# One float32 attention and mixture-of-experts layer: the first routed tile moved between two shared downs, and high-part products merged to 512 columns

## The reference, cut to what matters

```
x = x + attention(layernorm(x))
xt = layernorm(x).reshape(2048, 256)
topk_w, topk_i = top_k(sigmoid(xt @ w_router.T), 2)       # weights divided by their sum
gate = silu(einsum('th,eih->tei', xt, wg))
up = einsum('th,eih->tei', xt, wu)
expert_out = einsum('tei,ehi->teh', gate * up, wd)
out = einsum('te,teh->th', comb, expert_out)              # comb holds the weights
sgate = silu(einsum('th,jih->tji', xt, sg))
out = out + einsum('tji,jhi->th', sgate * einsum('th,jih->tji', xt, su), sd)
x = x + out
```

## Time and profile before

| | us |
|---|---|
| time, median of 3 runs | 905.71 (905.21 to 905.88) |
| the profiled execution | 906.11 |
| its span, first to last instruction | 904.4 |
| PE busy in the span | 870.5 (96%) |
| ACT, DVE, POOL busy | 578.6, 450.7, 276.2 |

### The profile page before, as it was taken

How to read it: one execution, slowest core, us unless ns; L and a number is a source line. 1 busy time by engine, 2 the same in 40 slices (tenths; PEclk the granted TensorE clock), 3 DMA queues, 4 the chain that set the end, 5 groups by cost and what they waited for, 6 DMA issues and landing times.

```text
span 904.4 us, 22574 instructions
## 1 busy us (share of the span) xinstructions
PE 870.5 (96%) x8167; PEld 561.6 (62%) x8168; DVE 450.7 (50%) x776; ACT 578.6 (64%) x733; POOL 276.2 (31%) x423
## 2 busy tenths in 40 slices
PE   8989999999999999999999999999999999999994
PEld 5524444433434343343447888888888989999983
DVE  8644443344444334454548677667834343434332
ACT  4789999999999999999993433342222222222220
POOL 5043334333333433333340000000024454544442
PEclk9979999999999999999999999999999999999998
DMA  6345444665544466733102206100037875575421
GB/s 189 122 132 185 151 164 164 218 214 210 193 154 162 161 219 228 244 99 90 31 13 76 70 27 240 50 1 24 1 101 217 269 226 160 158 205 154 121 36 23
DMA packets 42062, 124.43 MB, mean 138 GB/s; under 512 B 7668, under 2 KB 23028, under 8 KB 35824
## 3 DMA queue, kind: packets, MB, share of 16 engines
q1 hardware_dynamic: 31152, 110.35, 35.9%
q0 software_dynamic: 7072, 9.72, 6.0%
q10 hardware_dynamic: 3744, 3.02, 1.0%
HBM read 74.03 MB, written 49.02 MB: 136 GB/s over the span
## 4 chain that ended last, share of the span: by engine, by line
PE 79%; ACT 13%; issue 4%; DVE 2%; DMA 1%; POOL 0%; ACTq 0%; POOLq 0%; DVEq 0%
PE ps L1737 18%; PE ps L1910 14%; PE ps L1690 13%; PE ps L1864 12%; ACT arena L958 12%; PE ps L1932 7%; PE ps L1877 6%; PE ps L1921 2%; PE ps L1631 2%; PE ps L1791 2%; PE ps L1891 1%; DMA out<-arena,now_to 0%; PE ps L1821 0%; DMA xres<-x 0%; PE ps L1851 0%
## 5 line engine op out<-in xcount | busy, mean ns | idle before, releaser
L958 ACT ACTIVATE arena<-ps 128x1024 f32<-128x1024 f32 x336 | 319.9, 1063 | 2.0 <-PE ps L1690 2.0
L1737 PE MATMUL ps<-arena 128*32 128x256 f32 x4096 | 265.6, 386 | 0.6 <-POOL arena L785 0.6
L785 POOL TENSOR_SCALAR_AFFINE_SELECT arena<-arena 128x512 f32<-128x512 f32 x240 | 150.1, 638 | 265.7 <-ACT arena L969 258.0
L1690 PE MATMUL ps<-arena 64*128 64x512 bf16 (+1 forms) x1280 | 176.9, 343 | 12.1 <-ACT arena L958 8.5
L1737 PEld LDWEIGHTS ps<-arena 128*32 128x32 f32 x4096 | 112.4, 110 | 99.1 <-issue 42.4
L1690 PEld LDWEIGHTS ps<-arena 64*128 64x128 bf16 x1280 | 57.7, 94 | 157.9 <-ACT arena L958 79.5
L1189 DVE COPY_PREDICATED ps<-keep,ps 128x512 f32<-128x512 int32 (+1 forms) x128 | 80.6, 629 | 143.8 <-PE ps L1690 143.8
L1910 PE MATMUL ps<-wr_all,x2T 128*128 x648 | 141.3, 362 | 2.0 <-issue 1.0
L1910 PEld LDWEIGHTS ps<-wr_all,x2T 128*128 128x128 f32 x648 | 106.7, 189 | 19.5 <-issue 4.1
L1864 PE MATMUL ps<-x2T,wr_all 128*128 128x512 f32 x480 | 116.8, 394 | 1.3 <-issue 1.2
L969 ACT ACTIVATE arena<-ps 128x1024 f32<-128x1024 f32 x112 | 112.4, 1062 | 0.5 <-PE ps L1690 0.4
(11 more groups left out here) (198 smaller groups left out, 706.1 us busy)
## 6 DMA issues: line engine op xcount, KB each, us to landing
w_scr<-wr_all SPq DMA_DIRECT2D x24, 1280.0 KB, 7.3
wr_all<-w_scr SPq DMA_DIRECT2D x24, 1280.0 KB, 6.1
raw<-w_experts SPq DMA_DIRECT2D x24, 640.0 KB, 7.8
arena<-q_scr SPq DMA_DIRECT2D x64, 64.0 KB
o_scr<-arena SPq DMA_DIRECT2D x128, 32.0 KB, 1.7
arena<-o_scr SPq DMA_DIRECT2D x16, 256.0 KB, 4.0
raw<-w_shared SPq DMA_DIRECT2D x6, 640.0 KB, 5.0
q_scr<-parts SPq DMA_DIRECT2D x8, 384.0 KB, 3.0
```

What stands on the lines that cost most here:

```text
L785: nc.gpsimd.affine_select(out=dst, in_=src, compare_op=ALU.is_ge if own else ALU.is_gt, fill=0.0, base=0, pattern=[[0, REP], [-1 if own el ...
L958: nc.scalar.activation(prob[:, SLOT[unit(a, kt)], :, :].rearrange("p h q -> p (h q)"), score.rearrange("p b x -> p (b x)"), ACT.Exp, scale ...
L1690: return nc.tensor.matmul(ps[:, bank, :].rearrange("p (h q) -> p h q", h=2)[:, :, place * P:(place + tiles) * P], kst[r0:r0 + HALF, s, kt ...
L1737: last = nc.tensor.matmul(ps[32 * h:32 * h + 32, 6 + qc, a % 2 * QW:(a % 2 + 1) * QW], vst[:, s, kt, :], prob[:, SLOT[k], h, :], start=(no ...
```

## The change

- **Merged products.** In piece 2 (`SUMMED` = 1024 is its first column) and in the downs, the high activation part is multiplied with both weight parts in one product of 512 columns, whose moving operand is two pieces of 256 columns; the results lie side by side in the bank. The low activation part is multiplied with the high weights first, into the left half. So of three products of 256 columns one of 256 and one of 512 are left. The two halves are added on DVE: `up_sum` copies the left half to SBUF and adds the right one, for which `up` is cut in two; `y_out` scales the left half and then adds the scaled right half. The last tile's piece 2 and the last two tiles' downs stay as they were.
- **The first tile.** Pieces 0 to 2 of tile 0 and xT(1) stand between shared down(8) and down(9). Its hidden rows are turned into banks 3 and 6, since 4 and 5 still hold the shared downs; PE waits for the shared adds (`s_out`) only before hT(1). ACT's and DVE's steps for it move ahead too: DVE does `up` of tile 0 before it adds the last shared downs. `gact` and `hid` of parity 0 lie in another place of SBUF.
- **Chunk 0.** DVE copies the second half of the turned rows' high part, ACT only the first.
- **The last tile.** Piece 1 signals by itself, so `gate` can start before piece 2; `up` is cut in two with a wait for piece 2 between; the transposes signal in two parts.
- **POOL's `add`** waits for the scaled rows after it has staged the row numbers, read its count and waited for earlier adds. The pairs of ACT, DVE and POOL are written out, as PE's are.

```diff
             def add(j, i, p, n):
-                pool.wait_ge(e_y, j + 1 + FIRST)
                 stage(now_to[:, p:p + 1], slot_to[:, ds(j, 1)], n)
                 after = pool.value_load(tile_after[0:1, ds(j, 1)], min_val=16, max_val=16 * (NTILE // 2 + 1))
                 wait_apart(pool, e_added[1 - p], after)
+                wait_apart(pool, e_y, j + 1 + FIRST)
...
-            pairs = for_pairs(pool, 2, pair_rows)
...
             def x2_out(c):
                 act.wait_ge(c_tp, c + 1)
-                for k in range(KD):
+                for k in range(KD if c else 1):
                     nc.scalar.copy(x2T[:, 0, k, ds(c * CT, CT)], ps[:, XT_BANK[c] + k, :]).then_inc(c_xT, 1)
...
                     nc.scalar.activation(gsh[:, q % 2, :], ps[:, 2 * (q % 2), :], ACT.Silu).then_inc(s_act, 1)
+                    if step == NC * STEPS - 1:
+                        xT_out(0, 0)
                     act.wait_ge(s_hid, step + 1 + FIRST)
...
@@ -993,26 +998,28 @@
...
+            def hT_out(j, p):
+                act.wait_ge(e_th, j + 1)
+                if isinstance(j, int) and j == 0:
+                    nc.scalar.copy(hidT[:, 0, 0, 0:4].rearrange("p k t -> p (k t)"), ps[:, 3, :])
+                    nc.scalar.copy(hidT[:, 0, 0, 4], ps[:, 6, 0:P]).then_inc(e_hThi, 1)
+                    return
...
-            j = for_pairs(act, 1, pair) * 2 + 2
+            j = for_pairs(act, 1, pair, True) * 2 + 2
...
             gate(j + 1, 1)
-            act.wait_ge(e_th, j + 2)
             for i, (k0, k1) in enumerate(LAST_PARTS):
+                act.wait_ge(e_th, j + (2 + i))
...
+                if c == 0:
+                    nc.vector.tensor_copy(x2T[:, 0, 1, 0:CT], ps[:, XT_BANK[c] + 1, :]).then_inc(c_xT, 1)
...
+                    if step == NC * STEPS - 1:
+                        xT_low(0, 0)
...
                 if c == NC - 1:
-                    xT_low(0, 0)
+                    xT_low(1, 1)
+                    up_sum(0, 0)
+                    up(0, 0)
...
             def up(j, p):
                 dve.wait_ge(e_act, j + 1)
-                nc.vector.tensor_tensor(hid[:, p, :], gact[:, p, :],
-                                        ps[:, 0:3, :].rearrange("p b n -> p (b n)")[:, I:2 * I], ALU.mult) \
-                    .then_inc(e_hid, 1)
+                n = SUMMED - I
+                nc.vector.tensor_tensor(hid[p][:, 0:n], gact[p][:, 0:n], ps[:, 1, I - 512:I - 512 + n], ALU.mult)
+                dve.wait_ge(e_sum, j + 1)
+                nc.vector.tensor_tensor(hid[p][:, n:I], gact[p][:, n:I], hid[p][:, n:I], ALU.mult).then_inc(e_hid, 1)
+            def up_sum(j, p):
+                dve.wait_ge(e_gu, j + 1)
+                nc.vector.tensor_copy(hid[p][:, SUMMED - I:I], ps[:, 2, 0:2 * I - SUMMED]).then_inc(e_half, 1)
+                dve.wait_ge(e_half, j + 1)
+                nc.vector.tensor_tensor(hid[p][:, SUMMED - I:I], hid[p][:, SUMMED - I:I],
+                                        ps[:, 2, 2 * I - SUMMED:2 * (2 * I - SUMMED)], ALU.add).then_inc(e_sum, 1)
...
+                if isinstance(j, int) and j == 0:
+                    nc.vector.tensor_tensor(hidT[:, 0, 1, 0:4].rearrange("p k t -> p (k t)"), ps[:, 3, :],
...
-            def y_out(j, p):
+            def y_out(j, p, halves=False):
                 dve.wait_ge(e_mm, j + 1 + FIRST)
                 wait_apart(dve, y_free, j + 1)
+                if halves:
+                    nc.vector.tensor_scalar(ysb[:, p, :], ps[:, 6, 0:D], slot_w[:, ds(j, 1)], None, ALU.mult).then_inc(e_main, 1)
+                    dve.wait_ge(e_main, j + 1)
+                    nc.vector.scalar_tensor_tensor(out=ysb[:, p, :], in0=ps[:, 6, D:2 * D], scalar=slot_w[:, ds(j, 1)],
+                                                   in1=ysb[:, p, :], op0=ALU.mult, op1=ALU.add).then_inc(e_y, 1)
+                    return
...
             def routed_pair(i):
                 for p in range(2):
                     j = i * 2 + p
                     hT_low(j, p)
+                    up_sum(j + 1, 1 - p)
                     xT_low(j + 2, p)
                     up(j + 1, 1 - p)
-                    y_out(j, p)
-            j = for_pairs(dve, 1, routed_pair) * 2 + 2
+                    y_out(j, p, True)
+            j = for_pairs(dve, 1, routed_pair, True) * 2 + 2
...
-            up(j + 1, 1)
+            dve.wait_ge(e_act, j + 2)
+            n = 1024 - I
+            nc.vector.tensor_tensor(hid[1][:, 0:n], gact[1][:, 0:n], ps[:, 1, I - 512:512], ALU.mult)
+            dve.wait_ge(e_gu, j + 3)
+            nc.vector.tensor_tensor(hid[1][:, n:I], gact[1][:, n:I], ps[:, 2, 0:I - n], ALU.mult).then_inc(e_hid, 1)
...
-            def routed_up(p, slot, pieces):
+            def routed_up(p, slot, pieces, halves=True):
                 for n0, n in pieces:
+                    if n0 == SUMMED and halves:
+                        for k in range(KD):
+                            nc.tensor.matmul(ps[:, 2, 0:n], xsT[:, p, 1, k, :],
+                                             wr_all[:, ds(slot, 1), k, 0, n0:n0 + n].rearrange("p o n -> p (o n)"),
+                                             start=(k == 0), stop=(k == KD - 1), skip_group_check=True)
+                            last = nc.tensor.matmul(ps[:, 2, :].rearrange("p (w n) -> p w n", w=2), xsT[:, p, 0, k, :],
+                                                    wr_all[:, ds(slot, 1), k, :, n0:n0 + n].rearrange("p o w n -> p (o w) n"),
+                                                    start=False, stop=(k == KD - 1), skip_group_check=True)
+                        continue
...
             def routed_down(j, p, slot, parts=((0, KI),)):
                 pe.wait_ge(e_y, j + FIRST)
-                starts = {k0: i for i, (k0, _) in enumerate(parts)}
-                for k in range(KI):
-                    if k in starts:
-                        pe.wait_ge(e_hT, j + (starts[k] + 1 + FIRST))
+                for i, part in enumerate(parts):
+                    pe.wait_ge(e_hT, j + (i + 1 + FIRST))
+                    last = down_rows(p, slot, range(*part), parts == ((0, KI),))
+                last.then_inc(e_mm, 1)
+            def down_rows(p, slot, rows, halves=False):
+                for k in rows:
+                    if halves:
+                        nc.tensor.matmul(ps[:, 6, 0:D], hidT[:, p, 1, k, :],
+                                         wr_all[:, ds(slot, 1), 2, 0, k * D:(k + 1) * D].rearrange("p o n -> p (o n)"),
+                                         start=(k == 0), stop=(k == KI - 1), skip_group_check=True)
+                        last = nc.tensor.matmul(ps[:, 6, :].rearrange("p (w n) -> p w n", w=2), hidT[:, p, 0, k, :],
+                                                wr_all[:, ds(slot, 1), 2, :, k * D:(k + 1) * D].rearrange("p o w n -> p (o w) n"),
+                                                start=False, stop=(k == KI - 1), skip_group_check=True)
+                        continue
...
             def routed_rest(j, p, slot_next, half_next, between=lambda: None):
-                routed_hT(j, p)
+                if isinstance(j, int) and j == 0:
+                    routed_hT(0, 0, lambda k: (3, k) if k < 4 else (6, 0))
+                elif isinstance(j, int) and j == 1:
+                    pe.wait_ge(s_out, NC * TPC + FIRST)
+                    routed_hT(1, 1)
+                else:
+                    routed_hT(j, p)
...
                 shared_down(c, STEPS - 2)
+                if c == NC - 1:
+                    slot = slot_tile(0)
+                    pe.wait_ge(s_hid, NC * STEPS + FIRST)
+                    routed_up_first(0, 0, slot, later=False)
+                    routed_xT(1, 1, 0)
+                    routed_up(0, slot, PIECES[1:]).then_inc(e_gu, 1)
                 shared_down(c, STEPS - 1)
-                if c == NC - 1:
-                    routed_xT(1, 1, 0)
...
-            slot = slot_tile(0)
-            routed_up_first(0, 0, slot, later=False)
-            routed_up(0, slot, PIECES[1:]).then_inc(e_gu, 1)
             routed_up_first(1, 1, slot_tile(1))
...
-            pe.wait_ge(s_out, NC * TPC + FIRST)
             j = for_pairs(pe, 1, pair_of_tiles, True) * 2 + 2
-            slot_1, slot_0 = routed_rest(j, 0, lambda: slot_tile(j + 1), None, lambda: slot_tile(j))
-            routed_down(j, 0, slot_0)
-            routed_hT(j + 1, 1, lambda k: (4, k) if k < LAST_PARTS[1][0] else (5, k - LAST_PARTS[1][0]))
+            routed_hT(j, 0)
+            slot_1 = slot_tile(j + 1)
+            routed_up(1, slot_1, PIECES[1:2]).then_inc(e_gu, 1)
+            slot_0 = slot_tile(j)
+            routed_up(1, slot_1, PIECES[2:], halves=False).then_inc(e_gu, 1)
+            pe.wait_ge(e_y, j + FIRST)
+            pe.wait_ge(e_hT, j + (1 + FIRST))
+            down_rows(0, slot_0, range(KI)).then_inc(e_mm, 1)
+            pe.wait_ge(e_hid, j + 2 + FIRST)
+            for i, (k0, k1) in enumerate(LAST_PARTS):
+                for k in range(k0, k1):
```

(8 more changed lines are left out.)

24 lines of the change are left out of this document (12 added, 12 removed).

## The result

The changed kernel takes 901.17 us (median of 5 runs, 901.03 to 901.41), the kernel before 905.77 beside it (905.21 to 905.88): a ratio of 0.9952, 95% interval 0.9941 to 0.9964. Forecast were 901.2 and 4.5 us less; measured are 4.6 less. The total is right almost to a tenth, but its terms are not: one was 0.7 us too small, one had the wrong sign, one was counted though it is worth nothing, and they cancel. The rest of this document takes them apart.

The account below looks back on a forecast made before the run. PE's products were taken to bound the routed tiles. Terms 1.4 + 0 + 1.2 + 0.1 + 0.45 + 0.25 + 1.05 = 4.45 us, off the median of 905.71, gave 901.2 us; range 899.3 to 904.8.

Parts of the forecast that it names:

- PE bounds the routed tiles, and DVE's new work costs nothing: Routed tiles: PE's products set the time; DVE goes from about 2.5 to 4.1 of 6.05 us, costing nothing.
- the cover behind it: Steady tile, between DVE's low x and PE's next first piece: 0.39 us left, 0.2 counted as queue, so 0.19 spare.
- the rival: Routed tiles: slower copy and add delay the low x by 0.39 us, PE waits 0.2 a tile; 908.0 us, chance 9%.
- 1.4 us for the merge: Up piece 2 and downs of routed tiles: 240 merged triples save 6 ns each, 1.4 us.
- the bound of 2.2: Merged products: with 229 ns per wide product instead of 232, 9 ns saved per triple, 2.2 us in all.
- 1.2 us for the hole of the first tile: First routed tile: PE's wait for the gate is hidden under shared down products, 1.2 us saved, bounds 0.9 and 1.3.
- 0.1 less at the two slot numbers: Before 678.71 us, where PE's queue reads two slot numbers: the wait shrinks a little, 0.1 us.
- Chunk 0, 0.45: Start of chunk 0: DVE copies the second half beside ACT, so the low part starts 0.45 us earlier, bounds 0.3 and 0.5.
- The end, 0.25 + 1.05: Kernel's end: 0.25 us from the last transposes signalling in two parts, 1.05 from GpSimd preparing before its wait for scaled rows.
- (b): Kernel's end: GpSimd stages row numbers and reads its count before waiting for the scaled rows, 1.05 us saved.
- (a): Kernel's end: the last transposes signal in two parts, so ACT's first copy starts earlier, 0.25 us saved.
- the right case: Whole kernel: the forecast of 901.2 us holds, own range 899.7 to 902.4, chance 60%.

Follow-up runs that it names:

- the kernel with two copies: The changed kernel with two more copies of 256 columns on DVE per tile, ahead of the low x; 913.46 us.
- the kernel that keeps the numbers: The changed kernel in which PE keeps slot numbers already read, so each written-out pair reads two from the table, not four; 900.51 us.

## Why the prediction was right, and where it was not

- **PE bounds the routed tiles, and DVE's new work costs nothing:** right. The low x starts 1.01 us behind the gate against 1.00, and the cover behind it is 0.22 us by the kernel with two copies, against 0.19 counted. The prediction's price for the rival was a wait of 0.2 us when the low x starts 0.39 us late; 0.47 us late made 0.25, so the price was fair. Its condition, slower operations, did not come: copy and add take 0.42 each. What it left out is the multiply, which comes late first.
- **1.4 us for the merge:** the term that was too small. With 240 triples at 8.9 ns, by the two periods, it is 2.1 (2.02 us of it in the 32 periods). The wide product measures 232 as taken; 119 for a narrow one was fair too, but a difference of 6 ns out of two lengths that are rounded to 1 is uncertain by half, and the bound of 2.2, worked out with 229, was nearer. A part, about 13 ns a tile, is not in the triples at all. The page "TensorE: Matmul & The Clock Gate" of the Trainium skill, section "Back-to-back issue gap", would have given 0.6 us by its fixed 2.5 ns; the trace disagrees, with 7 ns in the triples themselves.
- **1.2 us for the hole of the first tile:** right, 1.22. The step that failed is the next one, **0.1 less at the two slot numbers**: it became 0.40 more. The prediction had the cause in hand, "the last row store of SyncE and the loads ... start some 4 us later", and costed that at nothing, as it asked only who waits for these transfers. It did not ask what they run beside: the store's burst moved onto a read of the slot table, which took 849 ns instead of 296 (that the store is the cause is inferred, as said above). It also took the bracket of 0.17 for the whole wait; 0.44 us were to be had there, as the kernel that keeps the numbers shows.
- **Chunk 0, 0.45:** the low products come 3.13 us behind the transposes instead of 3.58, 0.45; at the end of the shared stage 0.40 are left. No run takes this step back alone; in all 13 traces that have it, chunk 0 to the end of the shared ups takes 185.85 to 185.91 us, against 186.29.
- **The end, 0.25 + 1.05:** 1.06 in sum. For tile 34's add the step (b) is worth 1.03, as forecast. But the last add follows it by 3.86 us at least, by GpSimd's own work, so (a) is worth nothing and (b) is not counted twice. The prediction had this case ("(b) stays, since that add moves too, and (a) goes") with the wrong cause, the landing.
- **The sum:** +0.7 at the merge and -0.5 at the slot numbers, -0.25 at the end, -0.05 in chunk 0 make almost nothing. Behind the first mark the traces differ by 4.46 us, 4.45 forecast; attention adds 0.47 to that in the one pair of traces, and the medians differ by 4.60. The chances were for the right case, but that 901.2 was met to a tenth is luck. The range is not what its own terms give: with 2.2 for the merge, 1.3 for the hole, 0.5 for chunk 0 and 0.3 more for GpSimd and the start, its lower end is 900.0, not 899.3.

## What to carry to other kernels

Where a step is moved, look also at what its transfers and reads will lie beside, not only at who waits for them; here 0.40 of the 1.22 us that the move gained went that way. Before splitting or reordering the end of a kernel, write down the interval that each engine needs for itself between its last two steps: behind GpSimd's 3.87 us the 0.31 that DVE gained did not show. And where effects are below what a median resolves, compare intervals between fixed marks of two traces, and check with a second trace of the same kernel how far these repeat.

## What the runs showed of the hardware

- A product of fp32r with 512 moving columns costs 232 ns at the full granted clock, in a row with others, whether the columns lie in one piece or in two pieces 1280 columns apart; two of 256 cost 239 in their place.
- A read of a number in SBUF by PE's queue takes 0.30 us, 0.65 from one to the next, and 0.74 to 0.86 in the eight traces in which it begins with the burst of a store out of SBUF at some 350 GB/s. Elsewhere 8 of 882 reads take over 0.33, up to 0.76, all of them beside transfers. On GpSimd most such reads take 0.28 to 0.30; one that begins 1.94 us behind the start of GpSimd's own indirect DMA takes 0.38 (ten traces), and the longest took 0.80. The page "DMA: Bandwidth & Descriptors" of the Trainium skill, "Latency and other measured facts", gives a floor of about 0.6 us for such a load; here most reads take half of that, and the slow ones lie on both sides of it, 0.34 to 0.86.
- GpSimd needs 0.77 us from the end of the wait before an indirect DMA to its start, and with its preparation between the two, the last such DMA followed the one before it by 3.87 us in ten traces, also where DVE came 0.31 us later. In the old order of the add it was 3.70, with a long read of 0.61 in it. With the preparation ahead it followed within 3.38 and was still waiting for DVE.
- A wait of 0.25 us on PE showed no idle bracket, as modelled ends of products cover it; the distance of starts shows it.
